# Two row transfers under way at a time in the token dispatch of a four-stage network

## What is computed

```python
logits = x @ gate_weight.T                      # 64 experts
probs = softmax(logits)
top_val, top_idx = lax.top_k(probs, TOP_K)      # TOP_K = 8
...
flat_e = rerouted.reshape(-1)
order = jnp.argsort(flat_e)
tok = order // TOP_K
xs = x[tok]                                     # 16384 rows, sorted by expert
gu = lax.ragged_dot(xs, gate_up_proj, group_sizes)
...
y = lax.ragged_dot(hact, down_proj, group_sizes)
out = jnp.zeros_like(x).at[tok].add(y * w[:, None])
```

## Time and profile before

| | before |
|---|---|
| median of 3 runs | 2925.61 us (2925.49 to 2928.29) |
| span of the profiled execution | 2923.8 us |
| the profiled execution against the median | span 1.8 us below it |
| TensorE busy | 2490.2 us, 85% |
| VectorE busy | 1863.9 us, 64% |
| POOL busy | 1538.0 us, 53% |
| mean granted TensorE clock | 0.936 of full speed |

### The profile page before, as it was taken

The page is one execution under the profiler, slowest core; times in us unless marked ns, Lnnn a source line. Parts: engine busy times, 40 slices in busy tenths (PEclk is TensorE's granted clock), DMA queues, the critical chain, the costliest instruction groups (busy, mean ns, idle before and its releaser), DMA issues. The chain is left out here.

```text
span 2923.8 us, 42347 instructions
## 1 busy us (share of the span) xinstructions
PE 2490.2 (85%) x11348; PEld 1764.4 (60%) x11366; DVE 1863.9 (64%) x3083; ACT 1281.9 (44%) x2516; POOL 1538.0 (53%) x1262
## 2 busy tenths in 40 slices
PE   5998986597218699999999983999999999999797
PEld 2333432275216577777777762778777777877553
DVE  6999999865206544664444445775776676565586
ACT  4566664242106532322222211555555555555375
POOL 2656556323660166677666726774664665444122
PEclk8999999888659899999999995999999999999999
DMA  6989898635553499998778746443543543343101
GB/s 201 291 273 295 260 294 280 209 116 222 198 198 115 178 327 321 324 318 288 256 255 267 251 140 193 156 155 124 162 154 110 174 155 119 101 130 101 58 1 58
DMA packets 271499, 572.10 MB, mean 196 GB/s; under 512 B 26992, under 2 KB 92656, under 8 KB 270592
## 3 DMA queue, kind: packets, MB, share of 16 engines
q1 hardware_dynamic: 218080, 381.54, 39.6%
q0 software_dynamic: 44032, 167.80, 17.1%
q10 hardware_dynamic: 9248, 21.11, 2.1%
HBM read 361.69 MB, written 208.67 MB: 195 GB/s over the span
## 5 line engine op out<-in xcount | busy, mean ns | idle before, releaser
L624 POOL TENSOR_TENSOR b_u<-du,bc 128x1024 f32<-128x1024 f32 x128 | 300.9, 2351 | 214.7 <-DVE c_state L698 103.7
L450 PE MATMUL ps_y<-c_state,ident 128*128 128x512 f32 x512 | 255.1, 625 | 90.2 <-DVE c_state L698 90.2
L2002 ACT ACTIVATE prob<-ps_s,neg,q_rs 128x512 f32<-128x512 f32 x256 | 196.9, 773 | 264.1 <-DVE neg L2192 256.6
L689 DVE TENSOR_TENSOR_SCAN state<-ps_decay,b_u 128x1024 f32<-128x1024 f32 x128 | 292.7, 2287 | 14.6 <-POOL b_u L624 2.3
L1519 PE MATMUL ps_o<-w_dn,hid_t 96*128 x632 | 297.8, 593 | 0.0
L1555 ACT ACTIVATE silu_g<-ps_gu 128x192 f32<-128x192 f32 x159 | 52.5, 330 | 531.5 <-PE ps_gu L1500 531.5
L2096 POOL TENSOR_SCALAR prob<-prob,rden 128x512 f32<-128x512 f32 x256 | 174.6, 691 | 199.6 <-DVE rden L2200 199.6
L1500 PE MATMUL ps_gu<-w_gu_high,rows_t_high 128*128 (+1 forms) x636 | 228.2, 359 | 12.2 <-POOL w_gu_low L1385 10.8
L450 PEld LDWEIGHTS ps_y<-c_state,ident 128*128 128x128 f32 x512 | 92.8, 194 | 234.5 <-DVE c_state L698 143.9
L1385 POOL TENSOR_TENSOR w_gu_low<-raw_gu,w_gu_high 128x1536 fp32r<-128x1536 f32 x64 | 223.5, 3492 | 11.7 <-POOL w_gu_high L1383 11.7
L522 ACT ACTIVATE ps_decay<-delta,a_neg 128x511 f32<-128x511 f32 x256 | 165.7, 681 | 140.9 <-DVE state L689 139.7
(11 more groups left out here) (349 smaller groups left out, 6054.8 us busy)
## 6 DMA issues: line engine op xcount, KB each, us to landing
bc<-bc_dram SPq DMA_DIRECT2D x128, 512.0 KB
raw_gu<-in_gate_up POOLq DMA_DIRECT2D x64, 768.0 KB, 5.7
rows<-rows_dram SPq DMA_DIRECT2D x160, 256.0 KB, 4.7
y_dram<-y SPq DMA_DIRECT2D x158, 256.0 KB, 4.5
rows_dram<-zeros SPq DMA_DIRECT2D x46, 768.0 KB
w_q<-wq_dram SPq DMA_DIRECT2D x64, 512.0 KB, 3.6
w_o<-wo_dram SPq DMA_DIRECT2D x16, 2048.0 KB
w_dn<-in_down POOLq DMA_DIRECT2D x64, 384.0 KB, 6.1
```

The costliest lines, as they stand in the source:

```text
L450: mm = pe.matmul(ps_y[e][:, :], c.ident[:, :], c_state[:, q % 2, g, :], start=False, stop=False)
L624: pool.tensor_tensor(out=b_u[:, q % 2, :, :], in0=slot(du, n).rearrange("p (a l) -> p a l", a=1).broadcast_to([P, G, SEQ]), in1=bc[:, g % ...
L689: dve.tensor_tensor_scan(state[:, q % 2, :], decay[q % 2][:, :], b_u[:, q % 2, :, :].rearrange("p g l -> p (g l)"), 0.0, ALU.mult, ALU.add ...
L2002: act.activation(prob[:, qt, :], ps_s[qt % 2][:, :], ACT.Exp, scale=q_rs[:, k % 2, qt:qt + 1], bias=neg[:, qt:qt + 1], accum_out=den[:, qt ...
```

## The change

`send` begins with a wait: transfer n is issued when n // 2 transfers of its own parity (n - 2, n - 4 and so on) have landed. For that `m.sent` becomes two semaphores, one for even and one for odd n, and the wait at the end of `dispatch` becomes two. The helper `wait` leaves a wait out where the value is 0, so 126 waits are added. Nothing is reordered.

```diff
-EARLY = 26
+EARLY, FLYING = 26, 2
...
 def send(pool, m, n):
 
     k, t = n // NT, n % NT
+    wait(pool, m.sent[n % FLYING], 16 * (n // FLYING))
     return pool.indirect_dma_start(m.rows_dram, bass.IndirectOffsetOnAxis(ap=m.pos[:, k, t:t + 1], axis=0),
                                    m.xn[:, t, :], None)
...
             for n in range(EARLY):
                 if n % NT == 0:
                     pool_waits(pool, c, pos_made, n // NT + 1)
-                send(pool, m, n).then_inc(m.sent, 16)
+                send(pool, m, n).then_inc(m.sent[n % FLYING], 16)
...
             for n in range(EARLY, NT * TOPK):
-                send(pool, m, n).then_inc(m.sent, 16)
-            pool.wait_ge(m.sent, 16 * NT * TOPK)
+                send(pool, m, n).then_inc(m.sent[n % FLYING], 16)
+            for i in range(FLYING):
+                pool.wait_ge(m.sent[i], 16 * NT * TOPK // FLYING)
```

More of the change, by code:

```diff
@@ L2610, in program @@
                     q = Pipe(nc, first)
-                    m.raw_wk, m.wk_here, m.sent = q.sb("raw_wk", [P, KC, NH * HD]), q.sem("wk_here"), q.sem("sent")
+                    m.raw_wk, m.wk_here, m.sent = q.sb("raw_wk", [P, KC, NH * HD]), q.sem("wk_here"), [q.sem(f"sent{i}") for i in range(FLYING)]
                     route(nc, c, m, d)
```

## The result

| | before | changed |
|---|---|---|
| median of 4 runs | 2926.95 us (2925.49 to 2933.54) | 2835.12 us (2831.58 to 2839.08) |
| ratio | | 0.9694, 95% interval 0.9674 to 0.9714 |
| span of the profiled execution | 2923.8 us | 2837.6 us |
| mean granted TensorE clock | 0.936 | 0.948 |

The change gains 92 us; 60 were forecast. Two single runs of the kernel before in those later sessions, 6018.78 and 3245.67 us, lie far above all the others and are left out of every ratio.

The account below looks back on a forecast made before the run. Bound: a dispatch pause of some 115 us going with POOL's row transfers. At 2.0 us per transfer the experts start at about 944.7 instead of 1004.64 us, 60 us earlier: 2925.6 - 60 = 2865.6 us, range 2808 to 2946.

Parts of the forecast that it names:

- the forecast case: Dispatch: row-transfer period T of 1.6 to 2.5 us, total 2825 to 2918 us; chance 0.54.
- What bounds the kernel: Dispatch: some 115 us of pause going with POOL's row transfers, TensorE having 16.0 us of work in 115.3 us.
- The period: Row transfers, two under way: T = (L + 0.3) / 2, with issue-to-landing time L of 3.7 us, so 2.0 us.
- The first 26: Row transfers in the stage before dispatch: dispatch start kept at 737.95 us, with 9 us early and 3 us late allowed.
- The stage's end: Dispatch end on POOL: last landing 3.7 us after issue, about 1.0 us of stage change, experts at about 944.7 us.
- The k work as cover: Dispatch: k work ends at 884 to 891 us, over 50 us ahead of the last row transfer.
- The reason: Row transfers and stores: issued work that has not landed piles up, and everything going through memory stands behind it.
- not of what is under way, but of POOL's issuing as such: Rival, dispatch: pause lasts as long as POOL issues, 204 us and not 130; 72 us late, 2998 us; chance 0.08.
- one of the rivals: Row transfers: landing becomes the bound and is slow, L 5.8 us, T 3.05 us, 2991 us; chance 0.16.

## Why the prediction was right

The time (2835.1 us) lies in the range and in the forecast case's own (2825 to 2918), and the direction is the one forecast, on the kind of machine on which the kernel before was measured. Its accounting held better than its reason, and that is in part luck: the change helped because two landings take longer than the border of the pause, which no term of the prediction knew of.

- *What bounds the kernel* held. A pause goes with the row transfers, and it is worth what the stage gives back: TensorE's 16 of 115 us became 105 of 115 (755 to 870 us).
- *The period.* T = (L + 0.3) / 2 with L of 3.7 us gave 2.0 us; measured 1.71 us in the mean and 1.49 us when alone. L was mis-sized: 2.8 us quiet, and about 3.1 in the mean by the same formula, while the gathers of the earlier trace rows were taken for it. Over 101 transfers that is 101 x 0.29 = 29 us more gain. The quiet y store of 2.0 us with 0.65 us for POOL's longer issue (0.97 us, where SP's takes 0.32) would have been nearer. Of the 0.3 us from landing to issue, pairs of 2.98 us leave some 0.2 above an L of 2.8.
- *The first 26.* Taken as neutral; they lasted from 684.61 to 735.16, 50.6 us, instead of 60.7, since the v copies no longer paused. 10 us more gain, at the end that the text gave for it (9 us early).
- *The stage's end.* 3.7 us of landing and 1.0 us of stage change were charged; measured 12.1 us from the last issue to the experts (2.8 of landing and 9.3 of stage end on POOL). 7 us less gain. The 1.0 us was read where POOL had long been idle, and the change puts POOL last: the wrong row for it.
- Together 29 + 10 - 7 = 32 us, which is the difference between 60 and 92.
- *The k work as cover* held: the last k store was issued 141 us after the dispatch began (876.5), 143 to 150 were forecast.
- *The reason* was wrong: "work that was issued, and has not landed, piling up". With three under way the row transfers land within 3.8 us and the pause is there; with a pace and no waits for landings it isn't; with half the bytes it is. The landings of 15 to 23 us for v stores were upper bounds and no landings. ScalarE's copy at 704.63 stood still for 9.30 us, but from 699 to 705 us only the row transfers' queue moves packets: the data of the v stores, the last of them issued at 695.36, had gone. If the copy waited for a landing, it was the report that came late. And squares, which wait for no DMA, step in the same way. What the change really did was to stretch POOL's period over the border, because two landings happen to take longer than that. With three, which the reason called just as good (2795 to 2800 us), 0.4% is left of the gain.

```profile
DMA packets 377, 1.27 MB, mean 211 GB/s; under 512 B 68, under 2 KB 68, under 8 KB 377
q0 software_dynamic: 377, 1.27, 54.4%
```

- *The end of the pause* in the kernel before speaks against waiting row transfers too. The last one was issued at 867.98 us and no DMA packet moves from 870.5 to 877.4 us, but ScalarE still stands still until 877.41 and again until 882.28. ScalarE's long waits begin 12 to 16 us after POOL starts to issue in the dispatch, in every run with the pause, and in the five with transfers 1.27 us apart they end 12 to 14 us after its last issue. So something may well pile up, but it is neither the transfers nor their data, and no run shows what.

```profile
867.98:870.50 2.52, 0.00 (x0) 0.00 (x0) 0.00 (x0) 0.00 (x0) 0.96 (x1) 0.50 0.54 208
870.50:877.40 6.90, 0.00 (x0) 0.00 (x0) 0.00 (x0) 0.00 (x0) 0.00 (x0) 0.50 0.00 0
...
877.41 0.60 ACT L1223 ACTIVATE kv_sq<-ps_kk 128x512 f32<-128x512 f32 x1 [14.34 <-remote]
882.28 0.28 ACT L1228 ACTIVATE kv_sq<-ps_kk 128x128 f32<-128x128 f32 x1 [4.27 <-remote]
```

- *The rival "not of what is under way, but of POOL's issuing as such"*, at 0.08, came nearest to the cause; its consequence (a longer pause) was wrong, for it left out that the period between issues would change. "A cause that sits in one issue would act from the first" was the argument against it; the runs show that the pause goes with the closeness of issues, which shows itself after some.
- *The side on which it ends* was never a matter of the trace. Where there is no pause, the landing becomes the bound, as in one of the rivals, though it isn't slow: 1.73 us a transfer is enough to outlast the k work, and the change costs 51 us there. That the stretch before was a property of the session, and not of the program, couldn't be seen in one profile, and none of the chances allowed for it.

What stays open: what the engines wait for in a pause. It isn't the landing of a row transfer, nor bytes or packets, nor a branch. Every timed run here has a span from the profiler, so it isn't shown either that the pause is there when no trace is recorded. Nor was it tried whether issues of another kind (direct, or fewer rows each) do the same, or whether breaks help where there is a pause. And whether the two conditions belong to a chip or to where the program's memory comes to lie isn't settled; each session had one for all its runs in the ratios (20, 12, 7 and 7 of the kernel before), and never one between. The record numbers the chip 3 in the second session, without a pause, and in the last, with it; if that is one device, the condition isn't the chip's own.

## What to carry to other kernels

Where several engines stop together while GpSimd issues indirect DMAs back to back and the DMA engines are half idle, space the issues before limiting how many are under way: some 0.3 us of other work on GpSimd between transfers did at least as much here (0.965, 0.9625 to 0.9678) as waiting for landings with two under way (0.969, 0.9674 to 0.9714, in another session), and a limit of three or four did next to nothing. Take the kernel's time in more than one session before and after such a change: a remedy for a condition that isn't everywhere costs its price where the condition is absent (1.018). And when a change makes an engine the last of its stage, look for what its end of the stage costs; it was hidden before.

## What the runs showed of the hardware that was not expected

- One program has two times, 2774 to 2793 us and 2911 to 2934 us, by the session, and by the profiles the difference lies in the dispatch (144.3 or 266.7 us) and in the stage before (43.5 or 60.7 us up to the dispatch): TensorE is busy for 91.5 of 100 us, or for some 16, beside the same row transfers.
- In the slower condition indirect transfers of 128 rows 1.27 us apart hold up ScalarE by 10 to 16 us a step, at 1.36 us by 3 to 9 us, at 1.58 us not at all. Half the bytes, 113 GB/s, change nothing.
- Where POOL ends the dispatch, it takes 9.15 us from its last landing to its first instruction in the next stage, and neither an engine nor a DMA queue does anything in them. At the end of the stage before, where the kernel has no wait for landings, it takes 3.8 us from the end of POOL's last issue.
- An indirect transfer of 128 rows (256 KB) lands 2.7 to 4.7 us after its issue, 2.8 in the median, with two under way and no pause.
